# All one-hot bytes made in the second edge stage of a two-layer graph network, over groups 2 to 90, with three buffers

## What is computed

```python
def _egnn_conv(x, src, dst, edge_attr, W_msg, W_edge, W_root, b):
    msg = x[src] @ W_msg + edge_attr @ W_edge
    agg = jax.ops.segment_max(msg, dst, num_segments=x.shape[0])
    agg = jnp.where(jnp.isneginf(agg), 0.0, agg)
    return agg + x @ W_root + b

c1 = leaky_relu(_egnn_conv(x, src, dst, edge_attr, W1_msg, W1_edge, W1_root, b1))
c2 = leaky_relu(_egnn_conv(c1, src, dst, edge_attr, W2_msg, W2_edge, W2_root, b2))
return layernorm(x + c2)
```

## Time and profile before

| | us |
|---|---|
| median of three runs | 1830.65 (1825.43 to 1830.79) |
| the profiled execution | 1829.84 |
| its span, first to last instruction | 1828.0 |
| busy in the span: PE, DVE, ACT, POOL | 1518.9, 1277.1, 1068.6, 999.1 |
| mean granted clock of PE | 0.946 of full speed |

### The profile page before, as it was taken

One profiled execution on the slowest core, in us unless ns is written; L12 is line 12 of the kernel. 1 busy time (PEld: TensorE's weight loads), 2 busy tenths in 40 slices (PEclk: granted clock), 3 DMA queues, 4 the chain that ended last, 5 costly groups with the idle time before them and its releaser, 6 DMA issues.

```text
span 1828.0 us, 36625 instructions
## 1 busy us (share of the span) xinstructions
PE 1518.9 (83%) x11422; PEld 1354.1 (74%) x11422; DVE 1277.1 (70%) x1946; ACT 1068.6 (58%) x2402; POOL 999.1 (55%) x1454
## 2 busy tenths in 40 slices
PE   3999888989899999886999988988987766676664
PEld 2677777878789888885777777777787765675664
DVE  2665555555556555554899888888847888888887
ACT  2355555555534555663555555555538888888887
POOL 6777777777700000005777777777757555454443
PEclk9999999999999999997999999999999889878887
DMA  7769989888856788885888898888969999999997
GB/s 141 210 193 265 272 250 255 250 264 258 250 199 197 249 267 283 285 273 168 241 259 250 258 243 253 263 253 235 257 205 279 296 296 284 292 293 297 281 281 202
DMA packets 505019, 459.10 MB, mean 251 GB/s; under 512 B 348553, under 2 KB 412340, under 8 KB 504836
## 3 DMA queue, kind: packets, MB, share of 16 engines
q1 hardware_dynamic: 444118, 321.15, 62.2%
q0 software_dynamic: 30976, 57.72, 13.1%
q10 hardware_dynamic: 29742, 77.88, 10.9%
HBM read 283.25 MB, written 173.37 MB: 250 GB/s over the span
## 4 chain that ended last, share of the span: by engine, by line
PE 31%; POOL 30%; DMA 15%; issue 13%; ACT 7%; DVE 3%; SPq 1%; ACTq 0%; POOLq 0%; DVEq 0%
POOL arena_hold L419 28%; PE ps L597 20%; DMA out_dram<-arena_hold 7%; PE ps L508 4%; DMA arena_hold<-nodes,src_perm 4%; ACT arena_hold L776 3%; DMA arena_hold<-in_x_dram,src_all 3%; POOL onehot L454 2%; PE ps L474 2%; ACT ps L700 2%; PE ps L499 2%; ACT arena_hold L722 2%; PE ps L467 2%; DVE stats L1000 1%; DVE ps L983 1%
## 5 line engine op out<-in xcount | busy, mean ns | idle before, releaser
L597 PE MATMUL ps<-arena_hold,onehot 128*128 x4688 | 616.5, 295 | 166.5 <-POOL onehot L454 132.9
L597 PEld LDWEIGHTS ps<-arena_hold,onehot 128*128 128x128 f32 x4688 | 590.2, 208 | 193.1 <-issue 192.1
L419 POOL DMA_INDIRECT arena_hold<-nodes,src_perm x392 | 370.6, 945 | 448.7 <-SPq L384 329.5
L508 PEld LDWEIGHTS ps<-w_root,onehot 97*128 97x128 f32 x3136 | 399.1, 193 | 100.5 <-issue 97.0
L419 POOL DMA_INDIRECT arena_hold<-in_x_dram,src_all x392 | 377.2, 962 | 125.0 <-issue 115.5
L508 PE MATMUL ps<-w_root,onehot 97*128 97x128 f32 x3136 | 415.3, 275 | 0.0
L920 DVE TENSOR_TENSOR_SCAN arena_hold<-keep,arena_hold,ps 96x512 f32<-96x512 bf16 x196 | 248.5, 1268 | 209.1 <-PE ps L474 208.0
L661 ACT COPY arena_hold<-ps 128x384 f32<-128x384 f32 x392 | 187.9, 479 | 273.4 <-PE ps L508 270.5
L454 POOL CAST onehot<-keep 128x256 f32<-128x256 uint8 x588 | 209.6, 410 | 204.1 <-ACT ps L700 144.6
L934 DVE TENSOR_TENSOR onehot<-count,rel 128x1024 f32<-128x1024 bf16 x147 | 179.5, 1222 | 127.2 <-PE ps L597 123.2
L499 PE MATMUL ps<-ident,arena_hold 128*96 128x128 f32 x1568 | 240.8, 277 | 0.0
(11 more groups left out here) (97 smaller groups left out, 1147.1 us busy)
## 6 DMA issues: line engine op xcount, KB each, us to landing
root<-arena_hold ACTq DMA_DIRECT2D x196, 384.0 KB
arena_hold<-root SPq DMA_DIRECT2D x196, 384.0 KB, 4.0
nodes<-arena_hold SPq DMA_DIRECT2D x98, 384.0 KB, 3.0
arena_hold<-nodes SPq DMA_DIRECT2D x98, 384.0 KB
arena_hold<-in_x_dram SPq DMA_DIRECT2D x97, 384.0 KB
arena_hold<-in_x_dram SPq DMA_DIRECT2D x48, 768.0 KB, 9.1
out_dram<-arena_hold SPq DMA_DIRECT2D x48, 768.0 KB, 6.6
onehot_bytes<-arena_hold SPq DMA_DIRECT2D x147, 128.0 KB
```

The source lines that it names most:

```text
L419: nc.gpsimd.indirect_dma_start(out=gathered[t.ring][0:t.p, i, 0:D], out_offset=None, in_=table_in, in_offset=bass.IndirectOffsetOnAxis(ap= ...
L508: last = nc.tensor.matmul(no_ps[m % 2][:, i * P:(i + 1) * P], nodes_t[m % NODE_RING][0:D + 1, i * P:(i + 1) * P], w_root[0:D + 1, layer * ...
L597: nc.tensor.matmul(ps_bytes[:, bass.ds(place_at, SLOT)].bitcast(F32), onehot[:, k % NS, i, :], rows_from(t)[:, bass.ds(word, SLOT)].bitcas ...
```

## The change

All 147 batches of bytes are made in the second layer's edge stage, over its groups 2 to 89, as equally spread as whole batches allow. The buffers become three, each with its semaphore. The first edge stage no longer makes, stores or waits for bytes, and casts no count. To make room for the third buffer, the statistics of the norm (`stats`, `small`) are laid over `src_all`, which the second merge no longer needs.

```diff
-BYTES_AT = 15
+BYTE_RING = 3
 BYTES_ON = 2
 BYTES_OFF = 8
...
-    NBATCH_0 = NBATCH // 2
...
-        ARENA = max(2 * UNIT_RING * UB * D + (EDGE_RING + 4) * GE + 2 * BATCH * P // 4, UNIT_RING * UB * D + 5 * RI * D)
+        ARENA = max(2 * UNIT_RING * UB * D + (EDGE_RING + 4) * GE + BYTE_RING * BATCH * P // 4, UNIT_RING * UB * D + 5 * RI * D)
...
         src_all = sb("src_all", [P, NE * C], I32)
+        STATS, SMALL = RI // 2 * 6, 5 * RI
+        spare = src_all[:].bitcast(F32)
+        stats = spare[:, 0:STATS].rearrange("p (j c) -> p j c", c=6)
+        small = spare[:, STATS:STATS + SMALL].rearrange("p (i j) -> p i j", j=RI)
...
-        stats = sb("stats", [P, RI // 2, 6], F32)
-        small = sb("small", [P, 5, RI], F32)
...
-        bytes_stored, bytes_in = sems("bytes_stored"), sems("bytes_in")
+        bytes_stored, bytes_in = sems("bytes_stored", BYTE_RING), sems("bytes_in")
...
         def byte_batches(layer, g):
 
-            first, after = (BYTES_AT, NE) if layer == 0 else (BYTES_ON, NE - BYTES_OFF)
-            done, more = (0, NBATCH_0) if layer == 0 else (NBATCH_0, NBATCH - NBATCH_0)
-            span = after - first
-            return range(done + (g - first) * more // span, done + (g + 1 - first) * more // span) if first <= g < after else range(0)
+            span = NE - BYTES_OFF - BYTES_ON
+            return range((g - BYTES_ON) * NBATCH // span, (g + 1 - BYTES_ON) * NBATCH // span) if layer and BYTES_ON <= g < BYTES_ON + span else range(0)
...
             def store_bytes(k):
                 sp.wait_ge(bytes_made, k + 1)
-                sp.dma_start(onehot_dram[k // 2][:, k % 2 * BW:(k % 2 + 1) * BW], bytes_out[:, k % 2, :]).then_inc(bytes_stored[k % 2], DMA)
+                sp.dma_start(onehot_dram[k // 2][:, k % 2 * BW:(k % 2 + 1) * BW], bytes_out[:, k % BYTE_RING, :]).then_inc(bytes_stored[k % BYTE_RING], DMA)
...
-                if t.g == (BYTES_AT, BYTES_ON)[t.layer]:
-                    pe.wait_ge(count_set, t.layer + 1)
+                if t.layer == 1 and t.g == BYTES_ON:
+                    pe.wait_ge(count_set, 1)
                 if byte_batches(t.layer, t.g):
                     pe.wait_ge(bytes_made, byte_batches(t.layer, t.g).stop)
...
             def make_bytes(k):
-                if k >= 2:
-                    dve.wait_ge(bytes_stored[k % 2], DMA * (k // 2))
-                compare(bytes_out[:, k % 2, :].rearrange("p (t n) -> p t n", n=P), k, count_ps).then_inc(bytes_made, 1)
+                if k >= BYTE_RING:
+                    dve.wait_ge(bytes_stored[k % BYTE_RING], DMA * (k // BYTE_RING))
+                compare(bytes_out[:, k % BYTE_RING, :].rearrange("p (t n) -> p t n", n=P), k, count_ps).then_inc(bytes_made, 1)
...
-                    if g == (BYTES_AT, BYTES_ON)[layer]:
+                    if layer == 1 and g == BYTES_ON:
                         nc.vector.tensor_copy(count_ps, count[:]).then_inc(count_set, 1)
-                        dve.wait_ge(count_set, layer + 1)
+                        dve.wait_ge(count_set, 1)
```

More of the change, by code:

```diff
@@ L134, in gnn @@
         ring_bytes = keep[:].rearrange("p i n -> p (i n)").bitcast(U8).rearrange("p (i n) -> p i n", n=BW)
-        bytes_out = arena[:, at_rest + 4 * GE:at_rest + 4 * GE + 2 * BW // 4].bitcast(U8).rearrange("p (i n) -> p i n", n=BW)
+        bytes_out = arena[:, at_rest + 4 * GE:at_rest + 4 * GE + BYTE_RING * BW // 4].bitcast(U8).rearrange("p (i n) -> p i n", n=BW)
         def bytes_back(k, n):
@@ L262, in gnn @@
         dev, inv, shift = small[:, 0, :], [small[:, 1 + i, :] for i in range(2)], [small[:, 3 + i, :] for i in range(2)]
-        both = stats[:].rearrange("p j (h c) -> p j h c", c=3)
+        both = stats.rearrange("p j (h c) -> p j h c", c=3)
         mean, spread = both[:, :, :, 1], both[:, :, :, 2]
@@ L385, in _ @@
             edge_phase(1)
-            for i in range(2):
-                sp.wait_ge(bytes_stored[i], DMA * ((NBATCH + 1 - i) // 2))
+            for i in range(BYTE_RING):
+                sp.wait_ge(bytes_stored[i], DMA * ((NBATCH + BYTE_RING - 1 - i) // BYTE_RING))
             load_roots(1, 0)
@@ L438, in _ @@
                 gather(EdgeGroup(1, g))
-            for i in range(2):
-                pool.wait_ge(bytes_stored[i], DMA * ((NBATCH + 1 - i) // 2))
+            for i in range(BYTE_RING):
+                pool.wait_ge(bytes_stored[i], DMA * ((NBATCH + BYTE_RING - 1 - i) // BYTE_RING))
             pool.wait_ge(scanned, 2 * NE - 2)
```

## The result

| | before | after |
|---|---|---|
| median, us | 1830.65 (1825.43 to 1830.79) | 1850.42 (1849.28 to 1853.44) |
| ratio to before, 95% interval | | 1.013 (1.0112 to 1.0148) |
| profiled execution, span | 1829.84, 1828.0 | 1849.3, 1847.5 |

The change makes the kernel slower by 1.1 to 1.5%, and 1854.5 had been forecast. Against those the price is 1850.4 − 1826.8 = 23.6 us, which is the ratio of 1.013; against the median of the first few runs it is 19.8, a ratio of 1.011. The changed kernel itself was not timed again in those sets; its four runs are those of the table.

What follows compares the result with a forecast made beforehand. POOL's gathers, 5.0 us per group, were taken to bound both edge stages, with DVE pacing the second after the change. 1829.84 + 28.3 − 4.3 + 1 − 0.5 = 1854.3, said as 1854.5 us, range 1846 to 1876.

Steps and rivals of the forecast that it cites:

- POOL the clock before, DVE after: Second edge stage: POOL's gathers pace it at 5.0 us per group; after the change DVE does, at mean 5.32.
- The sum over groups 3 to 89: Second edge stage: 87 DVE turns with 146 batches take 462.9 us, ending 28.3 us later than before.
- The last eight groups: End of the second edge stage, no batches: PE paces at 4.29 us per turn, giving back 4.3 us.
- The stores: Second edge stage: batches waiting for the store three before cost +1 us, from 0 up to 27.
- the tight place: Two two-batch groups in a row, some 30 times: a store has 5.6 us to land, costing 0 to 0.9 us each.
- The first stage: End of the first edge stage: without its last compare the first load of root goes sooner, −0.5 us (0 to −1).
- The sum: Whole kernel: the profiled 1829.84 us plus all terms gives 1854.3, said as 1854.5 us.
- The signs: 870 to 1330 us: DVE over 95% busy, turns of 5.69 and 4.56, gathers released by PE; root load near 517.62.
- Store: Rival, second edge stage: stores landing in 6.5 us or more become the wait, 1881 to 1895 us; chance 0.10.
- Hidden: Rival, second edge stage: DVE's 46 us of idle time absorb the compares, 1830 to 1832 us; chance 0.05.
- Faster by freeing the gathers of the first stage: Rival, first edge stage: 73 fewer compares free gathers they held 0.94 us each, 68 us, to 1786; chance 0.04.
- PE's clock: Rival, second edge stage: PE's clock falls behind new gaps of about 1.4 us, 1899 to 1943 us; chance 0.05.

Runs made afterwards that it cites:

- narrow: The changed kernel, but from the eighth batch on every second compare writes one one-hot of eight, all stores kept; 1828.33 us, 1.001 of before.
- no_leaky: The changed kernel without the leaky ReLU of the node groups on DVE in the second layer, all compares kept; 1828.98 us, 1.0011 of before.
- split_110: The changed kernel with 37 batches made in the first edge stage and 110 in the second; 1828.00 us, 1.0003 of before.
- split_130: The changed kernel with 17 batches made in the first edge stage and 130 in the second; 1834.08 us, 1.0035 of before.
- ring of two: The changed kernel with two byte buffers in place of three; 1855.92 us, 1.0156 of before.
- off_4: The changed kernel with the batches spread over groups 2 to 93 in place of 89; 1853.21 us, 1.0143 of before.
- all_first: The changed kernel with all 147 batches made in the first edge stage, over groups 15 to 97; 1826.81 us, 0.9999 of before.
- count_sbuf: The changed kernel, but compares read the row of counts from SBUF in bf16 instead of the f32 copy in PSUM; 1962.51 us, 1.0776 of before.

## Why the prediction was right, step by step

**POOL the clock before, DVE after.** Right, and shown from both sides: less of DVE's work, of either kind, brings the time back (narrow, no_leaky), and the price starts where DVE's turn passes 5.0 us (split_110, split_130).

**The sum over groups 3 to 89.** 462.9 us of dense turns from 865.3 were forecast; L904 of group 4 came at 864.49 and that of group 91 at 1330.14, which is 465.65 us. Of the 2.75 more, 2.1 are the waits of two instructions (1.6 ahead of L904 and 0.5 ahead of L909) where 0.3 was allowed. Group 5 was ready later than in the trace of before, in a stage that had begun 1.5 us later:

```profile
864.49 0.68 DVE L904 TENSOR_TENSOR arena_hold<-ps,arena_hold 128x512 f32<-128x512 f32 x1
...
871.86 0.69 DVE L904 TENSOR_TENSOR arena_hold<-ps,arena_hold 128x512 f32<-128x512 f32 x1 [1.60 <-ACT arena_hold L639]
```

L904 of group 5 was let go at 871.86, not 871.28; after it the lag hid every late gather, as forecast. Against 1300.24 the shift is +29.9, forecast +28.3.

**The last eight groups.** −4.3 forecast. PE's turns (L466) run at 4.29 us as in the earlier trace rows (first and last of them):

```profile
1332.05 0.60 PE L466 MATMUL ps<-ident,arena_hold 128*128 128x128 f32 x4
...
1349.21 0.60 PE L466 MATMUL ps<-ident,arena_hold 128*128 128x128 f32 x4
...
1353.50 0.46 PE L466 MATMUL ps<-ident,arena_hold 84*128 84x84 f32 x4
```

The shift of group 97's turn is 1353.50 − 1327.77 = +25.7, so −4.2.

**The stores.** +1 was taken, with 27 as the far end. No compare in the profile after waited for a store, so the term is 0, and the ring of two showed that at this pace even 4.5 us is nearly always enough. The 27 us at the far end were too cautious for this kernel, though not without ground: in no_leaky 15 stores landed later than the 5.6 us of the tight place.

**The first stage.** −0.5 forecast (0 to −1). The first load of root was issued at 516.32 instead of 517.62, 1.3 us sooner, so outside the step's range and outside the 1 us that the prediction named as a sign. Nor is that move a result: over the profiles of the six kernels without bytes in the first stage this load was issued between 515.66 and 519.92, over the five with them between 516.63 and 520.59. POOL's first gather of the second stage came at 835.86, after 834.36 in the trace of before. Over the profiles that first gather came between 834.35 and 836.02 for five of the six kernels without bytes in the first stage (838.95 in off_4) and between 834.36 and 836.64 for those with them. An effect of half a microsecond can't be told there.

**The sum.** 1854.3 against 1849.3 in the profiled execution. The second edge stage grew by 24.5 us, where 28.3 − 4.3 + 1 = 25.0 was forecast, and it began 1.5 us later instead of 0.5 sooner; the rest, 6.5 us, is the second merge, which in that execution was shorter than in the profile of before by variation. That the stage came out within 0.5 us is in part luck: the waits that were set 1.8 us too low and the store that was set 1 us too high have opposite signs. Against the larger sets of runs of the kernel before the measured price (23.6 us) is within 1 us of the forecast 24.5, and it was the base, 1829.84 from a single execution, that lay some 3 us high.

**The signs.** L904 with almost no idle time, turns of 5.69 and 4.56 us, DVE busy over 95% and no idle time ahead of L933 (the old L934) all came as named. That gathers would be released by PE's turns "instead of issue" came only in part: 35 of the 363 waited for PE, 24.0 of 128.2 us, since DVE's turn is only 0.3 us longer than four gathers. The first load of root missed its sign, as said.

**The rivals.** Store: no wait seen. Hidden: the idle time took a good half and no more. From L905 of group 4 to that of group 91 (L904 after the change) DVE's instructions add up so: 72 more wide compares held it 79.0 us longer, its idle time, ahead of all its lines, fell by 45.1 us (47.3 to 2.25), its other instructions held it 3.8 us less, and the stretch grew by 79.0 − 45.1 − 3.8 = 30.1 us. (A compare with a wait behind it holds DVE for its whole 1.21 us, one without for 1.13; before, 31 of 73 had one.) Faster by freeing the gathers of the first stage: the 305 gathers of all_first from 120 to 500 us, beside 137 wide compares, took 944 ns, so these compares, with their row in PSUM, held up no gather. PE's clock: in the trace of before it did fall in the gap that the rival names, from a granted 1.00 to 0.50 (the trace holds no other value) at 856.9 us, 1.8 us into the 2.45, and it stood at 0.50 until 860.4; through the gap of 1.32 us ahead of 1314.55 it stayed at 1.00. After the change L485 waited 57 times for compares from 870 to 1330 us, 1.2 us each, and from 873 to 1367 us the clock granted was 1.00 throughout, against a mean of 0.98 before.

## What to carry to other kernels

In a stage paced by one engine, add up the other engines' work per step from start-to-start times in a dense stretch: work moved there is free up to the pace, and beyond it each step costs the excess, however much idle time the averages show elsewhere. Here about 122 of 147 batches would have fitted by this sum (110 were free, 130 cost 6.4 us), and the first stage had room for all of them. A price of a per cent or less needs the base from more than one execution: a merge that nothing touched moved by 8 us between profiles.

## What the runs showed of the hardware

A gather took as long however busy DVE was: 944 ns with DVE busy 36% of the time (after, 120 to 500 us), 945 with 89% (before, 860 to 1290 us) and 943 with 99.5% (after, 860 to 1330 us). It took longer with both inputs of the compare in SBUF (count_sbuf): 1338 ns on average from 860 to 1400 us, and 1.94 us where a compare overlapped it. On DVE, back-to-back instructions overlapped: a compare of 1.20 to 1.21 us held the engine for 1.13 when the next instruction was ready, so a sum of durations would have put 73 compares 6 us too high.
